# Expert weights split into parts during the attention, and two experts of the second batch added by scatters in DRAM instead of by 0/1 products

## What is computed

```python
probs = jax.nn.softmax(scores, axis=-1)
top_p, top_idx = jax.lax.top_k(jnp.transpose(probs, (0, 2, 1)), cap)   # cap = 256
xin = jnp.take_along_axis(x[:, None, :, :], top_idx[..., None], axis=2)
h = jax.nn.gelu(jnp.einsum('BElC,ECH->BElH', xin, w1), approximate=False)
y = jnp.einsum('BElH,EHC->BElC', h, w2)
y = y * top_p[..., None]
out = jnp.zeros((B, T, C), x.dtype).at[b_idx, top_idx].add(y)
...
x = _layernorm(x + out)
```

## Time and profile before

| | us |
|---|---|
| median of 3 runs | 909.22 (909.1 to 910.31) |
| the profiled execution, own time | 909.54 |
| its span in the profile | 907.8 |

### The profile page before, as it was taken

How to read it: one execution, slowest core, us unless ns; L and a number is a source line. 1 busy time by engine, 2 the same in 40 slices (tenths; PEclk the granted TensorE clock), 3 DMA queues, 4 the chain that set the end, 5 groups by cost and what they waited for, 6 DMA issues and landing times.

```text
span 907.8 us, 14912 instructions
## 1 busy us (share of the span) xinstructions
PE 866.8 (95%) x4598; PEld 729.4 (80%) x4598; DVE 692.2 (76%) x1163; ACT 748.7 (82%) x1449; POOL 639.6 (70%) x1031
## 2 busy tenths in 40 slices
PE   6889999999999999999999999999999999877995
PEld 5668888888888888888888888888888888776984
DVE  5777777777777777777777768778898787578675
ACT  3888898888888888888889888988888889665754
POOL 1777767667776777676778866667776677769782
PEclk9999999999999999999999999999999999979898
DMA  6010010101010101001010020000000001332233
GB/s 180 13 43 16 30 31 1 59 1 58 1 59 1 47 13 36 12 19 30 1 30 1 19 58 18 15 18 16 7 24 1 19 1 44 114 82 48 50 37 99
DMA packets 41663, 30.66 MB, mean 34 GB/s; under 512 B 5825, under 2 KB 39649, under 8 KB 41585
## 3 DMA queue, kind: packets, MB, share of 16 engines
q1 hardware_dynamic: 38256, 26.44, 9.7%
q0 software_dynamic: 3328, 3.28, 2.5%
HBM read 20.14 MB, written 9.57 MB: 33 GB/s over the span
## 4 chain that ended last, share of the span: by engine, by line
PE 81%; POOL 6%; DVE 5%; issue 4%; ACT 2%; DMA 1%; POOLq 0%; SPq 0%; DVEq 0%; ACTq 0%
PE t_ps L1580 11%; PE ring_a L1541 6%; PE ring_a L1543 6%; PE ring_a L1542 6%; PE ring_b L1541 6%; PE ring_b L1543 6%; PE u_ps L1541 6%; PE ring_b L1542 6%; PE u_ps L1543 6%; PE u_ps L1542 6%; PE o_ps L1541 2%; PE o_ps L1542 2%; PE o_ps L1543 2%; PE x_ps L1541 2%; PE x_ps L1543 2%
## 5 line engine op out<-in xcount | busy, mean ns | idle before, releaser
L640 POOL TENSOR_TENSOR attn<-prob 128x1024 f32<-128x1024 f32 x128 | 307.4, 2402 | 173.5 <-ACT prob L799 161.8
L1056 DVE TENSOR_TENSOR at_lo<-t_ps,at_hi 128x512 fp32r<-128x512 f32 x253 | 174.1, 688 | 100.7 <-ACT at_hi L782 100.4
L1049 DVE TENSOR_REDUCE negmax<-ring_a 128x1 f32<-128x1024 f32 x128 | 156.7, 1224 | 58.6 <-PE ring_a L1543 55.7
L782 ACT ACTIVATE at_hi<-t_ps 128x512 fp32r<-128x512 f32 x253 | 151.6, 599 | 39.8 <-PE t_ps L1580 38.7
L1049 DVE TENSOR_REDUCE negmax<-ring_b 128x1 f32<-128x1024 f32 x128 | 156.2, 1220 | 2.7 <-PE ring_b L1543 1.1
L1580 PE MATMUL t_ps<-ident,attn 128*128 128x128 f32 x1012 | 152.1, 272 | 4.3 <-DVE at_lo L1056 4.1
L799 ACT ACTIVATE prob<-prob,coef 128x1024 f32<-128x1024 f32 x128 | 147.6, 1153 | 5.7 <-POOL coef L604 5.6
L1580 PEld LDWEIGHTS t_ps<-ident,attn 128*128 128x128 f32 x1012 | 124.4, 140 | 30.0 <-DVE at_lo L1056 9.4
L793 ACT ACTIVATE prob<-ring_a,negmax 128x1024 f32<-128x1024 f32 x128 | 143.1, 1118 | 4.6 <-DVE negmax L1049 4.1
L793 ACT ACTIVATE prob<-ring_b,negmax 128x1024 f32<-128x1024 f32 x128 | 142.4, 1112 | 0.6 <-DVE negmax L1049 0.5
L1541 PE MATMUL ring_b<-xt_hi,q_hi 128*128 128x512 f32 x256 | 112.0, 438 | 0.0
(11 more groups left out here) (450 smaller groups left out, 1792.6 us busy)
## 6 DMA issues: line engine op xcount, KB each, us to landing
attn<-in_L_ffn_w SPq DMA_DIRECT2D x12, 256.0 KB, 3.3
ww_dram<-ww_hi SPq DMA_DIRECT2D x8, 192.0 KB, 2.5
ww_dram<-ww_lo SPq DMA_DIRECT2D x8, 192.0 KB, 2.9
ww_hi<-ww_dram SPq DMA_DIRECT2D x8, 192.0 KB, 2.4
ww_lo<-ww_dram SPq DMA_DIRECT2D x8, 192.0 KB, 2.5
wq_s<-in_L_attn_Wq SPq DMA_DIRECT2D x8, 128.0 KB, 2.7
wk_s<-in_L_attn_Wk SPq DMA_DIRECT2D x8, 128.0 KB, 3.1
xres<-in_L_attn_X SPq DMA_DIRECT2D x2, 512.0 KB, 6.3
```

Source lines behind the costliest of these rows:

```text
L640: pool.tensor_tensor(attn[:, t % AB, :], prob[:, t % 2, 1, :], prob[:, t % 2, 0, :], ALU.add).then_inc(attn_ready, 1)
L782: act.activation(at_hi[:, g % 2, half * GT:(half + 1) * GT, c], t_bank(t, half)[:, :].rearrange("p (k q) -> p k q", q=P), ACT.Copy).then_i ...
L1049: dve.tensor_reduce(negmax[:, par, m:m + 1], ring[m][:, :], axis=AX.X, op=ALU.max, negate=True).then_inc(negmax_ready, 1)
L1056: dve.tensor_tensor(at_lo[:, g % 2, k, c], t_bank(t, half)[:, :].rearrange("p (k q) -> p k q", q=P), at_hi[:, g % 2, k, c].bitcast(F32), A ...
```

## The change

Four things are altered together.

1. **Weights split in the attention.** In tiles 8 to 71 SP loads each expert's w1 and w2 in turn into one buffer (`keep_parts`), POOL rounds it (`w_round`) and subtracts (`w_lower`) in tiles 3, 4, 6 and 7 of each eight, and SP stores both parts to DRAM (`w_parts`). In the tail SP reads finished parts (`load_parts`), 1 MB an expert instead of 0.5 MB, and ACT, DVE and POOL split no weights there.
2. **g_lo of the first 14 halves on POOL.** ACT writes the whole Gelu into SBUF (`g_full`, four buffers) instead of PSUM, and POOL subtracts (`g_lower`). Scatters 0, 1 and 2 stand behind subtractions 6, 8 and 10, and the gathers of the second batch behind subtraction 13.
3. **Jobs 8 and 9 are scattered.** The second batch's x1 is stored to `acc_x1`; scatters 8 and 9 add into it, each behind the landing of the scatter before it; SP reads it back over x1 before `add_mixed`. `mix` and `one_hots` are made for six experts instead of eight.
4. **TensorE's order.** 26 products that nobody reads (`idle_work`) stand between the first steps of the tail, and halves 12 and 13 are moved between `limit`, `offset` and `tokens`. ACT loads the Gelu table behind `rows_copy` instead of ahead of it.

```diff
+    WSEM = 2
+    NP = 14
+    SC = 2
...
+        raw_w, raw_hi = raw_a[:, 0:F], raw_a[:, F:2 * F].bitcast(F32R)
+        g_full = [attn[:, 2 + n // 2, n % 2 * NC:(n % 2 + 1) * NC].rearrange("p (f c) -> p f c", c=CAP)
+                  for n in range(HOTS)]
...
+            def keep_parts(e):
...
+                    need(sp, w_kept, 32 * c)
+                    sp.dma_start(raw_w.rearrange("p (f c) -> p f c", f=FT), v).then_inc(w_raw_in, 16)
+                    sp.wait_ge(w_split, c + 1)
+                    for part, t in enumerate((raw_hi.bitcast(F32), raw_w)):
+                        sp.dma_start(w_parts[e, part][:, w * F:(w + 1) * F], t).then_inc(w_kept, 16)
...
+                if 2 <= k < E + 2:
+                    keep_parts(k - 2)
...
+            sp.wait_ge(scores_ready, 2 * TILES)
+            for e in range(E // 2):
+                load_parts(e)
+            store_x1(1)
...
+            for n in range(2):
+                sp.wait_ge(scattered[n], 16 * CT * (E + SC) // 2)
+            sp.wait_ge(xg_stored[1], 16)
+            for h in range(2):
+                sp.wait_ge(x2_in[h], 32)
+                s = slice(h * GT, (h + 1) * GT)
+                sp.dma_start(x1[:, QT:2 * QT, :][:, s, :],
+                             acc_x1.rearrange("(t p) d -> p t d", p=P)[:, s, :]).then_inc(x2_in[h], 16)
...
                 pool.wait_ge(y_scaled, y_count(q))
+                if q >= E:
+                    pool.wait_ge(acc_stored, 32)
+                    need(pool, scattered[(q - 1) % 2], 16 * CT * ((q + 1) // 2))
...
+            def g_lower(n):
+
+                q, f = n // 2, slice(n % 2 * 2, n % 2 * 2 + 2)
+                pool.wait_ge(g_hi_done, n + 1)
+                pool.wait_ge(gelu_ready, n + 1)
+                pool.tensor_tensor(g_lo[q % 2][:, f, :], g_full[n % HOTS], g_hi[q % 2][:, f, :].bitcast(F32),
+                                   ALU.subtract).then_inc(g_split, 1)
...
+                if QT <= G < (E + 1) * QT:
+                    e, s = G // QT - 1, G % QT
+                    if s in (3, 6):
+                        w_round(e, s // 6)
+                    if s in (4, 7):
+                        w_lower(e, s // 7)
...
+            for n in range(NP):
+                g_lower(n)
+                if n in (6, 8, 10):
+                    scatter((n - 6) // 2)
             gather_ready(1)
...
-            for q in range(2, E):
+            for q in range(3, E + SC):
                 scatter(q)
...
+            dve.wait_ge(x2_in[h], 48)
...
-                if q < JOBS:
+                if q < JOBS and n >= NP:
...
+            pe.wait_ge(y_added, 122)
+            idle_work(ring[0][:, 0:WWN], 4)
             x1_transposes(1, 0)
+            idle_work(ring[0][:, 0:WWN], 6)
             rows_in(0)
+            idle_work(ring[0][:, 0:WWN], 2)
             x1_transposes(1, 1)
...
+            down(last - 2)
             limit(1)
+            rows_in((last + 1) // 2 + 1)
+            up(last + 1)
             offset(1)
+            up(last + 2)
             tokens(1)
             counts(1, 0)
             counts(1, 1)
-            for n in range(last + 1, 2 * JOBS + 2):
+            rows_out((last + 2) // 2 - 2)
+            down(last - 1)
+            for n in range(last + 3, 2 * JOBS + 2):
```

More of the change, by code:

```diff
@@ L358, in y_count @@
         def y_count(q):
[L360 removed]
+            return q + 1 + min(q + 1, E + SC)
         def exists(t):
@@ L476, in _ @@
                     load_ww(k)
[L478 to L491, removed]
+            sp.wait_ge(w_kept, 64 * E)
+            sp.wait_ge(scores_ready, 2 * TILES)
+            for e in range(E // 2):
+                load_parts(e)
+            store_x1(1)
+            store_pn(1)
+            store_rows(1)
+            load_vals(1)
+            sp.wait_ge(u_ready, 31)
+            for e in range(E // 2, E):
+                load_parts(e)
             for n in range(2):
@@ L665, in scatter @@
                 pool.wait_ge(y_scaled, y_count(q))
+                if q >= E:
+                    pool.wait_ge(acc_stored, 32)
+                    need(pool, scattered[(q - 1) % 2], 16 * CT * ((q + 1) // 2))
+                    for k in range(CT):
+                        pool.indirect_dma_start(out=acc_x1, out_offset=where(q, k), in_=yr[q][:, k, :],
+                                                in_offset=None, bounds_check=N - 1,
+                                                compute_op=ALU.add).then_inc(scattered[q % 2], 16)
+                    return
                 need(pool, scattered[q % 2], 16 * CT * (q // 2))
@@ L715, in _ @@
             norm(115)
-            for n in range(2, 7):
+            for n in range(2, 8):
                 gather_rows(n // CT, n % CT)
             norm_end(END)
-            for n in range(7, 9):
+            for n in range(8, 11):
                 gather_rows(n // CT, n % CT)
@@ L838, in signs @@
                                bias=slot_neg[:, h:h + 1]).then_inc(sgn_ready, 1)
-            def w_round(e):
-                for w in range(2):
-                    if w == 0:
-                        act.wait_ge(w_in[e], 32)
-                    act.activation(w_hi[e][:, w], raws[e][:, w], ACT.Copy).then_inc(w_hi_done, 1)
             def xs_round(q):
@@ L870, in ffn @@
                     act.activation(yt[q % 2], dn_ps, ACT.Copy).then_inc(yt_copied, 1)
-                if half == 1 and 0 <= q - 2 < E:
+                if half == 1 and 0 <= q - 2 < E + SC:
                     y_scale(q - 2)
@@ L1349, in ffn @@
                 y = q - 2
-                if half == 1 and E <= y < JOBS:
+                if half == 1 and E + SC <= y < JOBS:
                     dve.wait_ge(y_ready, y + 1)
-                    need(dve, mix_done, y - E - 1)
+                    need(dve, mix_done, y - E - SC - 1)
                     hi, lo = y_mix[y % 2]
@@ L1877, in mix @@
                                                one_hot[m % HOTS][k][:, h * NC:(h + 1) * NC],
-                                               start=(m == 0 and k == 0 and part == 0),
+                                               start=(m == SC and k == 0 and part == 0),
                                                stop=(m == E - 1 and k == CT - 1 and part == 1))
@@ L1905, in ffn, with idle_work @@
                     up(n)
+            def idle_work(dst, count):
+                for _ in range(count):
+                    pe.matmul(dst, ww_hi[:, 1, 0:P], ww_hi[:, 1, 0:WWN], start=True, stop=True)
+            pe.wait_ge(y_added, 122)
+            idle_work(ring[0][:, 0:WWN], 4)
             x1_transposes(1, 0)
+            idle_work(ring[0][:, 0:WWN], 6)
             rows_in(0)
+            idle_work(ring[0][:, 0:WWN], 2)
             x1_transposes(1, 1)
```

105 lines of the change are left out of this document (49 added, 56 removed).

## The result

The changed kernel takes 927.16 us (median of 4 runs, 924.88 to 928.78) where the kernel before took 909.56 beside it: a ratio of 1.0191, 95% interval 1.0163 to 1.0219. It is slower, as forecast. The forecast of 920.7 was 6.5 us short, and the median lies 0.2 us above the upper end of the range, 927. Taken by the ratio, on the 909.22 that the prediction started from, it is 926.6, inside that range; the forecast's own range, 916 to 926, it misses either way. The profiled execution took 925.75 us, its span is 923.8.

A forecast was written before the change was run, and what follows sets the result against it. Bound by TensorE to about 797, DVE's counting levels to 842, POOL's queue to 893. First gather at 851.4 plus 69.6 gives 921.0, put at 920.7 for the median; own range 916 to 926, with rivals 912 to 927.

The forecast's parts named there:

- the attention: Tiles 8 to 71: POOL's copies and subtractions fit its idle time and cost zero, at worst 5 us.
- last tile to first count: Start of the tail: second norm_end about 0.9 us late, while the count may start a microsecond earlier.
- first count to first gather: Counting levels: POOL's scatter pairs and subtractions delay the second batch's first gather from 842.15 to 851.4, +9.2 us.
- first gather to addition: POOL's second-batch gathers, five scatter pairs, serial experts 8 and 9, and the acc_x1 read sum to 57.6 us.
- The rival of POOL's splits on the path: Attention: POOL's weight splits reach the path, 5 us on top, 925.7 us; chance 0.08.
- TensorE gaps in tiles 8 to 71: Attention: a sign that the prediction is wrong; no size given.
- 849 to 854: Tail: the second batch's first gather starting in this span is a sign that the prediction is right.
- their microsecond: Start of the tail: idle products hold the clock; without that the levels start where they did, 1 us.
- no worse than before: Counting levels up to half 6: POOL's subtractions cost nothing more, subtraction 6 ends at the old 825.8.
- The rival with hidden scatters: Levels: scatters hide while TensorE has other work, first gather 3.8 us later, total 915.2 us; chance 0.12.
- TensorE's saving: Second batch's mixing: two experts fewer give back 4.2 us of TensorE, off the path.
- The rival in which TensorE's shorter stream sets the end: Tail: levels at DVE's own 2.4 us, POOL's chain ends at 892.6, total 904.3 us; chance 0.05.

The follow-up runs named there:

- e1: The changed kernel with SyncE issuing load_ww(8) behind keep_parts(7), not ahead of it: 923.48 us.
- e5: The kernel before with only experts 8 and 9 of the second batch scattered into acc_x1: 916.93 us, ratio 1.0075.
- e2: The changed kernel with SC = 0, experts 8 and 9 mixed by TensorE's products again, no acc_x1: 924.02 us.
- e6: The changed kernel with NP = 0: VectorE makes g_lo again, first three scatter pairs stand ahead of the gathers: 917.02 us.
- e10: The kernel of e7 run again, beside e9 and the kernel before: 909.52 us, ratio 0.9982.
- e3: The changed kernel with its first three scatters moved from between POOL's subtractions to behind the gathers: 933.28 us.
- e7: The changed kernel with the edits of e1, e2 and e6 together: 908.7 us, ratio 0.9979.
- e8: The changed kernel with expert 8's scatter pair waiting for expert 6's landing, not expert 7's: 925.56 us.
- e4: The changed kernel without the 26 idle products of TensorE: 929.33 us.
- e9: The kernel of e7 with seven more idle products late in the attention and one gather fewer ahead of each norm_end of POOL: 908.0 us, ratio 0.997.
- e11: The kernel of e9 without any of its 33 idle products: 910.53 us, ratio 0.9994.

## Why the prediction was right, and where it was short

Taken along the profiled execution (forecast 921.0 on that scale, measured 925.75):

| step | forecast us | measured us |
|---|---|---|
| the attention | 0, bound 5 | +4.7 (tile 127's combine 778.57 to 783.30) |
| last tile to first count | about 0 | -0.8 (29.85 to 29.08) |
| first count to first gather | +9.2 | +9.7 (33.73 to 43.39) |
| first gather to addition | 57.6 | 57.85 |
| addition to the span's end | 10.3 | 10.2 |
| around the span | 1.7 | 1.95 |

- **The attention at zero** is the step that failed, and it is nearly the whole error. The last `combine`, before and then changed:

```profile
778.57 2.39 POOL L640 TENSOR_TENSOR attn<-prob 128x1024 f32<-128x1024 f32 x1 [1.21 <-ACT prob L799]
783.30 2.39 POOL L673 TENSOR_TENSOR attn<-prob 128x1024 f32<-128x1024 f32 x1 [2.55 <-ACT prob L842]
```

By the starts of this instruction the changed kernel is 0.6 us ahead at tile 0 (the start, which lies 0.8 ahead to 1.0 behind in the other executions), and then loses 1.7 from tile 11 to 32, 2.3 at tile 67 and 1.3 at tile 127: together 4.7.

- *Tile 67* is the order of SyncE (e1). The sentence "SP's waits for the parts come two tiles ahead of the loads that are queued behind them, so these cost nothing" looked only at what stands behind those waits. What stands ahead was not looked at: `load_ww(8)` holds the raw load of `keep_parts(7)` back until POOL has nothing to split.
- *Tiles 11 to 32.* POOL's time sufficed, but a subtraction on POOL stretched one on VectorE. In tiles 23 and 31 VectorE splits the second batch's input (`xt_lo`) just then. Tile 23, changed and then before:

```profile
150.80 1.30 POOL L722 TENSOR_TENSOR raw_a<-raw_a 128x512 fp32r<-128x512 f32 x1
151.30 1.35 DVE L1079 TENSOR_TENSOR xt_lo<-xg,xt_hi 128x512 fp32r<-128x512 f32 x1
153.40 0.47 PE L1571 MATMUL u_ps<-at_hi,xk_hi 128*128 128x512 f32 x1 [0.92 <-DVE u_lo L1099]
```

```profile
151.56 0.68 DVE L1042 TENSOR_TENSOR xt_lo<-xg,xt_hi 128x512 fp32r<-128x512 f32 x1
152.99 0.47 PE L1541 MATMUL u_ps<-at_hi,xk_hi 128*128 128x512 f32 x1 [0.25 <-DVE u_lo L1062]
```

VectorE takes 1.35 us instead of 0.68, u_lo comes behind it, and TensorE waits 0.67 longer, twice: 1.3 of the 1.7. It is so in all eleven traces with the splits and in neither of the two without; no run moved the subtraction, and what the other 0.4 is stays open. The prediction compared POOL's instruction with POOL's idle alone. From 300 to 400, and in e1 from 400 to 500, the splits cost TensorE nothing, as argued.

- *Tile 127* goes with a granted clock of 0.55 and 0.60 from 778 to 782, where the kernel before has 1.00. In the eight executions in which the clock fell there, e5 with the old attention among them, this tile adds 0.7 to 1.4 us; where it stayed, nothing. So this part, like the 0.6 at the start, is the luck of the execution.

The rival of POOL's splits on the path, 925.7 at a chance of 0.08, had the time nearly right, but of its 5 us only the 1.3 of tiles 23 and 31 came about, by another way. "TensorE gaps in tiles 8 to 71" was one of the prediction's own signs of being wrong; they came. The first gather, 855.77, also lies behind the 849 to 854 of its signs of being right; the attention's 4.7 account for that.

- **The last tile to the count**: norm_end(120) was late by 0.5 us rather than 0.9 (its row starts at 799.74, 5.2 later than in the earlier trace rows, of which 4.7 come from the attention). That the idle products gave their microsecond here is not shown: with them the same stretch is 29.05 to 29.10 us in four traces (the changed kernel, e2, e6, e10) and 30.24 to 30.30 in four others (e1, e3, e7, e8), without them 30.91 in e4; 28.63 in e9 stands against 29.95 in e11.
- **The levels**: the mechanism was right, votes behind halves that wait for POOL behind scatter pairs. Two things were off and nearly cancel. The first subtractions wait behind gathers and the iota, and VectorE's second step already waits 2.41 us (819.00), since TensorE waits 2.70 us for the first subtraction (817.24), where the forecast said "no worse than before" up to half 6. On the other side the two long late waits of TensorE are 2.56 and 2.17 us, not 3, and the second of them is half 13's, behind the levels. The rival with hidden scatters falls by e3: 8.0 us for three pairs, where they occupy POOL for 11.
- **The first gather to the end** was right in each term: the late pairs start 5.96 us apart (forecast 5.95), and the read and the addition follow 2.9 us behind. The Trainium skill, DMA: Bandwidth & Descriptors, section "Anatomy of one DMA — SWDGE (gpsimd) path", would have made each landing about 2.15 us, an estimate from that page; the trace shows 3.84, 3.28 and 3.29, and the measurement decides.
- **TensorE's saving** is off the path, as said: its mixing ends 49.9 us behind the first gather, 8 us ahead of the addition. The rival in which TensorE's shorter stream sets the end has a true half: without scatters between them the levels take 23.99 us (e3), less than the 25.51 of before. It never comes to bear, since POOL stays late for the gathers: subtractions 12 and 13 stand ahead of them, and from the last step to the gather it is 11.45 us in e3 and 8.22 in the kernel before.
- **The range** was too short at its top, since with the bound of 5 us taken in full beside the rest it would have ended past 930; I counted the two as rivals, and they add.

## What to carry to other kernels

When work is put into an in-order queue, read what stands ahead of it as well as behind: one load behind a foreign wait cost 3.7 us here, and moving one line gave them back. Work belongs on an engine with idle time only if its place in that engine's order is early enough: 1.3 us subtractions behind 3.7 us scatter pairs were worse than the same subtractions on the busier VectorE. And idle time on the one engine is not all: look at what the neighbour runs at that moment; beside a subtraction of POOL, one of VectorE took twice as long here, and TensorE waited for it. A chain of dependent scatters costs a landing each; two of them took 12 us in place of 4.2 us of products that had a place beside other work.

## What the runs showed of the hardware

VectorE's instructions with two inputs in SBUF took longer beside a subtraction of POOL. In the attention xt_lo took 1.35 us instead of 0.68, twice in each of the eleven traces with the splits, and that reached TensorE (rows above). In the tail a short scan took nine times as long. The two scans of the changed kernel:

```profile
843.31 0.29 DVE L1312 TENSOR_TENSOR_SCAN prob<-prob 128x64 f32<-128x64 f32 x1
844.75 2.68 DVE L1329 TENSOR_TENSOR_SCAN prob<-prob 128x64 f32<-128x64 f32 x1
```

The second ends at 847.43, right behind POOL's subtraction (845.46 + 1.81 = 847.27). It is 2.68 us too in e1, e2, e4 and e8, whose POOL has the same order, and 0.29 in e3 and e6. A scatter alone does not do it: in the kernel before the scan took 0.29 us inside one.

```profile
836.18 1.56 POOL L668 DMA_INDIRECT acc_dram<-prob,idx  x1 [0.31 <-issue]
836.48 0.29 DVE L1299 TENSOR_TENSOR_SCAN prob<-prob 128x64 f32<-128x64 f32 x1
```

The profile puts the start of POOL's subtraction 0.71 us behind that of the long scan, so which came first is not clear from these rows; in tile 23 POOL's comes first by 0.50. The Trainium skill, SBUF — State Buffer, section "SBUF: two separate sides", has VectorE with two SBUF inputs and a reading GpSimd exclude each other for a whole instruction; the ends in these rows agree with it. In the tail the time was hidden, as far as the rows show: TensorE's half 13 waited for that same subtraction until 847.33, and the token product came behind it at 848.78.
